# Cross-attention block: x plus the output bias formed ahead, during the projections, and kept in DRAM

## The reference, cut to what matters

```python
# x: (4, 512, 512) float32, ctx: (4, 512, 512), mask: all true, 16 heads of 32
residual = x
xn = layer_norm(x, ln1_w, ln1_b)
q = xn @ q_w + q_b ; k = ctx @ k_w + k_b ; v = ctx @ v_w + v_b
attn = softmax(where(mask, q @ k.T / sqrt(32), min))
out = (attn @ v) @ cproj_w + cproj_b
hidden = out + residual
y = layer_norm(hidden, ln2_w, ln2_b)
y = gelu(y @ fc_w + fc_b) @ proj_w + proj_b
return hidden + y
```

## Time and profile before

| | |
|---|---|
| device time, median of 3 runs | 771.24 us (770.92 to 771.43) |
| span of the profiled execution, first to last instruction | 769.3 us |
| PE busy | 744.1 us (97%) |
| DVE busy | 457.1 us (59%) |
| POOL busy | 299.1 us (39%) |
| ACT busy | 281.4 us (37%) |

### The profile page before, as it was taken

How to read it: one execution, slowest core, us unless ns; L and a number is a source line. 1 busy time by engine, 2 the same in 40 slices (tenths; PEclk the granted TensorE clock), 3 DMA queues, 4 the chain that set the end, 5 groups by cost and what they waited for, 6 DMA issues and landing times.

```text
span 769.3 us, 10036 instructions
## 1 busy us (share of the span) xinstructions
PE 744.1 (97%) x3664; PEld 514.2 (67%) x3664; DVE 457.1 (59%) x995; ACT 281.4 (37%) x492; POOL 299.1 (39%) x183
## 2 busy tenths in 40 slices
PE   7999999989999999999999999999999999999998
PEld 5878886733344444444436888888888888888886
DVE  6673347778888888898697668443424333232213
ACT  4534241276766566667682011211112111211110
POOL 2654150068998778798754002212002200220000
PEclk9999999999999999999999999999999999999999
DMA  9656377597666785678641537240220413030001
GB/s 328 231 167 214 136 220 240 193 268 167 158 164 146 184 216 145 156 209 177 176 136 53 181 109 202 74 165 0 42 69 18 147 18 93 1 109 1 1 0 55
DMA packets 94385, 103.25 MB, mean 134 GB/s; under 512 B 39968, under 2 KB 48420, under 8 KB 94336
## 3 DMA queue, kind: packets, MB, share of 16 engines
q1 hardware_dynamic: 94192, 102.59, 46.5%
q10 hardware_dynamic: 144, 0.02, 0.0%
HBM read 73.08 MB, written 29.37 MB: 133 GB/s over the span
## 4 chain that ended last, share of the span: by engine, by line
PE 80%; DVE 12%; issue 3%; ACT 2%; DMA 1%; POOL 1%; SPq 0%; ACTq 0%; DVEq 0%
PE ps L487 22%; PE ps L488 21%; PE ps L489 21%; DVE ps L1009 6%; PE ps L594 4%; PE ps L610 4%; PE ps L579 4%; PE ps L625 3%; DVE R L1144 2%; ACT Pt L797 1%; PE ps L547 1%; DVE mx L1009 1%; DMA qs<-BIG 1%; DVE R L945 1%; DVE st L932 1%
## 5 line engine op out<-in xcount | busy, mean ns | idle before, releaser
L797 ACT ACTIVATE Pt<-ps 128x512 f32<-128x512 f32 x256 | 137.6, 598 | 70.9 <-PE ps L594 69.6
L1178 DVE CAST HR<-R 128x512 fp32r<-128x512 f32 x52 | 24.9, 478 | 186.0 <-ACT R L832 186.0
L832 ACT ACTIVATE R<-ps,cols 128x512 f32<-128x512 f32 x52 | 35.9, 690 | 227.2 <-PE ps L489 227.1
L594 PE MATMUL ps<-BIG 98*128 98x512 f32 x256 | 93.2, 439 | 3.6 <-ACT Pt L797 3.2
L1009 DVE CUSTOM_DVE_ANT_0 ps<-ps,FU 128x512 f32<-128x512 f32 x128 | 84.6, 724 | 14.9 <-PE ps L579 14.8
L1009 DVE CUSTOM_DVE_ANT_0 ps<-ps,BIG 128x512 f32<-128x512 f32 x128 | 84.6, 723 | 10.8 <-PE ps L579 10.7
L594 PEld LDWEIGHTS ps<-BIG 98*128 98x128 f32 x256 | 44.2, 187 | 68.3 <-issue 29.3
L487 PE MATMUL ps<-BIG,HR 128*128 128x512 f32 x192 | 74.8, 390 | 1.0 <-DVE HR L1180 1.0
L487 PE MATMUL ps<-YT,BIG 128*128 128x512 f32 x192 | 74.9, 390 | 0.0
L488 PE MATMUL ps<-YT,BIG 128*128 128x512 f32 x192 | 74.7, 389 | 0.0
L489 PE MATMUL ps<-BIG,HR 128*128 128x512 f32 x192 | 74.7, 389 | 0.0
(11 more groups left out here) (132 smaller groups left out, 1371.3 us busy)
## 6 DMA issues: line engine op xcount, KB each, us to landing
BIG<-qs SPq DMA_DIRECT2D x62, 256.0 KB, 2.8
BIG<-ks SPq DMA_DIRECT2D x62, 256.0 KB, 3.2
ks<-BIG SPq DMA_DIRECT2D x32, 256.0 KB, 2.0
qs<-BIG SPq DMA_DIRECT2D x32, 256.0 KB, 5.8
R<-hd SPq DMA_DIRECT2D x28, 256.0 KB, 3.9
R<-in_x SPq DMA_DIRECT2D x16, 256.0 KB, 5.4
hd<-R SPq DMA_DIRECT2D x16, 256.0 KB, 3.2
yt<-FU SPq DMA_DIRECT2D x64, 64.0 KB, 1.9
```

The source lines that it names most:

```text
L594: eng.matmul(bk, K_[0:98, j, kc * 128:(kc + 1) * 128], Q_[0:98, j, :], start=True, stop=True).then_inc(S["p_ra"], 1)
L797: eng.activation(Pt[:, r, j % 2, :], bank(bank_a(("s2", i, j))), ACT.Exp, scale=SCALE).then_inc(S["a_ra"], 1)
L832: eng.activation(g, bank(4 + i % 2), ACT.Gelu_apprx_tanh, bias=fcb[:, f:f + 1]).then_inc(S["a_g"], 1)
L1178: eng.tensor_copy(HR[:, n, 0, :], g).then_inc(S["v_hh"], 1)
```

## The change

GpSimd no longer adds the bias in the attention for batches 0 to 2. Instead, in the projections, SP loads x of batch b into `V[:, 12:16, :]`, GpSimd adds `cbt` there in place, and SP stores the four chunks in a new DRAM tensor `xc`. In the attention, SP loads `R2[:, c, :]` from `xc` instead of from x, and DVE's first addition waits for that load alone. Batch 3 keeps the old way.

```diff
+        xc = nc.dram_tensor("xc", (3, 4, 128, 512), F32, kind="Internal").ap()
@@ sync
+            def load_ahead(b):
+                for c in range(4):
+                    if b:
+                        sp.wait_ge(f"d_xs{c}", 16 * b)
+                    eng.dma_start(V[:, 12 + c, :], xv[b][:, c, :]).then_inc(S[f"d_xl{c}"], 16)
+
+            def store_ahead(b):
+                for c in range(4):
+                    sp.wait_ge("g_xs", 4 * b + c + 1)
+                    eng.dma_start(xc[b, c], V[:, 12 + c, :]).then_inc(S[f"d_xs{c}"], 16)
@@ sync, loop over the batches
             for b in range(B):
                 if b == 3:
                     load_stack(1)
+                if b == 1 or b == 2:
+                    load_ahead(b - 1)
                 for g in range(4):
                     store_qk(b, g, 0)
+                if b == 1 or b == 2:
+                    store_ahead(b - 1)
                 if b == 3:
                     load_lead(2)
                 if b == 2:
                     load_lead(0)
                     load_mask(0)
                     load_lead(1)
+                    load_ahead(2)
                     load_stack(0)
...
                 for g in range(4):
...
+                    if b == 2 and g == 1:
+                        store_ahead(2)
@@ sync, attention
-                            eng.dma_start(R2[:, c, :], xv[n][:, c, :]).then_inc(S[f"d_xr{c}"], 16)
+                            if n < B - 1:
+                                sp.wait_ge(f"d_xs{c}", 48)
+                            eng.dma_start(R2[:, c, :], xc[n, c] if n < B - 1 else xv[n][:, c, :]).then_inc(S[f"d_xr{c}"], 16)
@@ scalar, eviction of V
                     act.wait_ge("p_pj", 12 * b + c + 1)
+                    if b == 3:
+                        act.wait_ge(f"d_xs{c}", 48)
@@ vector, first half of an output projection
-                        dve.wait_ge("g_xc", 4 * n + c + 1)
+                        dve.wait_ge(f"d_xr{c}", 16 * (n + 1))
@@ gpsimd
+            def add_ahead(b):
+                pool.wait_ge("d_cb", 16)
+                for c in range(4):
+                    pool.wait_ge(f"d_xl{c}", 16 * (b + 1))
+                    eng.tensor_tensor(V[:, 12 + c, :], V[:, 12 + c, :], cbt[:, :], ALU.add).then_inc(S["g_xs"], 1)
@@ gpsimd, projections
             for b in (2, 3):
                 root(b % 2, b)
+                add_ahead(b - 2)
+                if b == 3:
+                    add_ahead(2)
                 ctx_low(b)
                 x_low(b)
@@ gpsimd, attention
-                for n in range(B - 1):
-                    for c in range(4):
-                        if i == 16 * n + 14 + 2 * c:
-                            x_add(n, c)
```

More of the change, by code:

```diff
@@ L138, in cross_attention_block @@
                      "v_t2", "a_sh", "v_at", "v_ac", "v_sh", "v_sl", "v_hh", "v_hl", "v_o", "v_cp",
-                     "g_rs", "g_lo", "g_xl", "g_ac", "g_al", "g_xc", "g_sl", "g_hb", "g_ql", "g_at", "g_wc", "v_nb",
+                     "g_rs", "g_lo", "g_xl", "g_ac", "g_al", "g_xc", "g_xs", "g_sl", "g_hb", "g_ql", "g_at", "g_wc", "v_nb",
                      "d_vec", "d_m8", "d_mk", "d_on", "d_cb", "d_pb", "d_wc", "d_m"):
             S[name] = ctx.enter_context(nc.semaphore("s_" + name))
-        for name, n in (("d_st", 3), ("d_qk", 4), ("d_xr", 4), ("d_hd", 4), ("d_h", 4), ("d_hb", 4), ("d_o", 4), ("d_w", 2), ("d_hi", 2), ("d_mb", 4), ("d_ys", 4), ("d_yl", 4)):
+        for name, n in (("d_st", 3), ("d_qk", 4), ("d_xr", 4), ("d_xl", 4), ("d_xs", 4), ("d_hd", 4), ("d_h", 4), ("d_hb", 4), ("d_o", 4), ("d_w", 2), ("d_hi", 2), ("d_mb", 4), ("d_ys", 4), ("d_yl", 4)):
             for i in range(n):
@@ L467, in _ @@
                 if i == 6:
-                    sp.wait_ge("g_xc", 16)
+                    sp.wait_ge("g_xc", 4)
                     eng.dma_start(cbt[:, :], pj_b.partition_broadcast(128)).then_inc(S["d_pb"], 16)
@@ L1193, in _ @@
                     dve.wait_ge("p_cp", c + 1)
-                    dve.wait_ge("g_xc", 12 + c + 1)
+                    dve.wait_ge("g_xc", c + 1)
                     eng.tensor_tensor(R2[:, c, :], bank(6 + i % 2), R2[:, c, :], ALU.add).then_inc(S["v_cp"], 1)
@@ L1249, in divide_c @@
                 eng.tensor_tensor(prod(s), copied(s), R1[:, 2, :], ALU.mult).then_inc(S["g_at"], 1)
+            def add_ahead(b):
[3 more added lines that the diff above has]
+                    eng.tensor_tensor(V[:, 12 + c, :], V[:, 12 + c, :], cbt[:, :], ALU.add).then_inc(S["g_xs"], 1)
             def x_add(b, c):
-                pool.wait_ge("d_cb", 16)
                 pool.wait_ge(f"d_xr{c}", 16 * (b + 1))
```

## The result

The changed kernel takes 781.69 us (median of 4 runs, 781.23 to 782.76) against 771.34 us for the kernel before (4 runs, one more than in the table above): 1.0138 of before, 95% interval 1.0126 to 1.0150, 10.35 us slower. The profiled execution has a span of 780.9 us, 11.6 more than the one of before, and is the longest of its four.

The account below looks back on a forecast made before the run. PE was taken to hold the end (80% of the chain of waits); a 6.1 us stall plus 2.3 us of slow clock made 8.4 us, span 769.3 to 777.7, 779.6 with the 1.9 us around it; range 776.0 to 785.0.

Parts of the forecast that it names:

- Nothing gained in the attention: Attention: removing twelve GpSimd additions, 15.5 us of its time, gains 0; at best 0.3 us, or 1 us.
- Batches 0 and 1 covered: Projections: the loads, additions and stores added for batches 0 and 1 are hidden and cost 0.
- `add_ahead(2)` holds `ctx_low(3)`: Batch 3's projections: GpSimd's additions, waiting for a late load, delay `ctx_low(3)` from 103.29 to 117.7 us, and PE waits.
- The length of the stall, 6.1 us: Before batch 3's V: PE, wanting the first half of `ctx_low(3)` at 114.06 us, resumes at 120.2, 6.1 us later.
- my own rival of later loads: Loads for batch 2: added SP transfers make chunks land like the slow loads, +11 to +14 us, 784; chance 0.15.
- The clock, 2.3 us: After PE's gap before batch 3's V: the first twelve matmuls run at half clock and cost 2.3 us more.
- The rival in which PE keeps its clock: Batch 3's V: no slow matmuls, stall 6.1 + 0.9 = 7.0 us, 778.2; chance 0.14.
- ACT's wait for the store of chunk 0: Batch 3's V: `store_ahead(2)` lands its last chunk by 122.6 us, before ACT wants the first at 125.4; 0, at worst about 1.
- one of the prediction's own signs of being wrong: Listed: PE gap under 4 us, matmuls at 0.227 behind it, ACT waiting on `xc` stores, or attention shorter by some us.
- the bounds worked out: Whole cost: +5.3 us with landing 2.6 and unchanged clock; +14.3 with landing 8.6, additions up to 1.73 and slow clock.

Follow-up runs that it names:

- the change of order: The changed kernel with `ctx_low(3)` ahead of `add_ahead(2)` in GpSimd's order: 771.88 us, 1.0020 of the kernel before.
- the filler: The changed kernel with 36 matmuls of 128x512, result unread, on PE right ahead of batch 3's V: 781.14 us, 1.0134 of the kernel before.
- the variant with the sooner load: The changed kernel with `load_ahead(2)` ahead of the two lead loads and the mask in SP's queue: 777.08 us, 1.0076 of the kernel before.

## Why the prediction was right, and where it was not

The forecast was 779.6 us, the measured median 781.69; the mechanism and its place are those forecast, and the range held the time. Two transfers were priced too low: one made the stall too short, the other was called covered and was so only by luck.

- *Nothing gained in the attention.* Right, taken as 0, measured -0.06 us, within 0.7, by the variant without the additions.
- *Batches 0 and 1 covered.* Right, shown by the variant with these alone.
- *`add_ahead(2)` holds `ctx_low(3)` and this PE.* Right, shown by the change of order, which takes back 10 of the 11 us.
- *The length of the stall, 6.1 us.* Too short by 3.7 us, in two terms of the sum. `store_ahead(1)` was given four issues of 0.35 us, by rows of single stores; four in a row took 3.07 us here, 2.60 to 3.43 in the other variants. And the landing was taken as 4.3 us, that of the lead loads themselves; the load behind them took 6.6, and 5.8 to 6.4 in the three other traces with the same queue. I had put the loads at the price of their neighbours, when the neighbours are what they queue behind. That is the mechanism of my own rival of later loads, at about half its price: the profiled 11.6 us are inside the 11 to 14 that it gave, the medians between it and the forecast. The rest is the additions, which waited 0.7 us for their later chunks, less 0.8 for the leads, issued in 2.5 us instead of 3.3, and 0.2 for additions that ran a little faster.
- *The clock, 2.3 us.* Right in size, 4.83 us for what takes 2.49 at the upper level, and right in hiding the second half of `ctx_low(3)`. The rule of the Trainium skill, page "TensorE: Matmul & The Clock Gate", section "HAM oscillation — how this bites in real kernels", agrees with the 0.50 in the row. The rival in which PE keeps its clock is out by that row and by the filler.
- *ACT's wait for the store of chunk 0, "covered".* Wrong, and one of the prediction's own signs of being wrong. The store was issued at 117.69 us, when it was forecast, but took 11.2 us to land instead of 3.5, longer than the 7.9 of the bound. ACT evicted at 128.98, released by it in the trace, 0.3 us after PE's last matmul of the chunk had ended (128.09 + 0.59). That PE lost nothing here is luck: the stall that was longer than forecast had made PE as late as the store. In the reordered variant this same wait cost PE 1.5 us. I had priced it by the median of the earlier trace rows, and those rows hold two kinds. By the traced order of SP's queue, the four stores issued within 1 us behind an operand stack (at 248.57, 265.10, 313.91 and 330.29 us) took 6.4, 7.9, 6.0 and 7.3 us to land; the other eight took 2.0 to 5.2. `store_ahead(2)` stands behind a stack.
- *The median and the profile.* Worked out against the profiled span, 8.4 us; the profile shows 11.6 and the medians 10.4 to 11.4. The ends of the range, +4.8 and +13.8, don't follow from the bounds worked out, +5.3 less 0.3 to 1 for the attention and +14.3; the measured time lies well inside either.

## What to carry to other kernels

An engine that is nearly idle in a stage may still be on the path at one instruction there: before moving work onto it, find in the order of time what stands behind the new work and who waits for that, and how long the new work's own input takes to come. Here the busy share, 39%, and the slack of 8 us both looked ample, and the queue ahead of the load used them up. Taking work off an engine is worth what others wait for it, here 0.3 us at most, whatever its busy share. And price a transfer by its place in the queue, not by the median of its like.

## What the runs showed of the hardware

- **A short gap can cost the clock after PE has resumed.** In the variant with the sooner load, PE stood still for 3.07 us, ran six matmuls 0.23 apart, stood for 0.69 us, and only then ran at 0.50, for 15 matmuls. The clock column reads 1.00 from 116.45 to 117.80 us and 0.50 from 117.90 on, so it fell while PE was running the sixth. By stretch, the gap, the six, the slow ones:

```profile
113.30:116.40 3.10, 0.08 (x1) 0.00 (x0) 0.75 (x1) 0.69 (x1) 3.10 (x3) 1.00 0.91 283
116.45:118.10 1.65, 1.65 (x6) 1.01 (x6) 0.00 (x0) 0.00 (x0) 1.65 (x1) 0.93 1.07 180
118.83:124.50 5.67, 5.67 (x15) 3.81 (x16) 2.01 (x7) 0.00 (x0) 4.79 (x4) 0.50 1.06 281
```

  One of its six runs kept a mean clock of 1.000 and was the fastest, 775.16 us; the others had 0.995 to 0.998 and 776.78 to 778.42. So after such a gap the clock seems to fall in some executions and not in others; the fastest run is 1.6 to 3.3 us below the rest. Only one of the six has a trace, so that the gap was as long in the fastest isn't shown; and one of the 23 runs of the kernel before on this chip also has a lower mean clock, 0.997, and 773.94 us.
- **The landing of a 256 KB load** in this place was 2.5 to 4.2 us with no load ahead in the queue, 5.9 to 6.4 behind the leads with the stack moved away, and 5.2 to 9.5 behind the leads and with the stack following. The first chunk seems to be set by what stands ahead (5.9 us without the stack, 5.2 to 6.6 with it), the last by what follows too (at most 6.4 without it, 6.8 to 9.5 with it). A store of `xc` of batch 1 or 2 was 2.0 to 4.3 us where no stack had been issued ahead, and 9.2 to 11.4 with it.
- **The printed clock is not complete.** At the kernel's start it says 1.00 over matmuls that are 0.435 us apart; in the changed kernel's middle it says 0.50 over matmuls 0.43 apart.
- Why four stores in a row take SP 2.6 to 3.4 us to issue, where single ones took 0.33, stays open.
